# Three convolutions and an expert layer on one core: first image by ScalarE alone, group sums a pair later, scales ahead of the last low part, stores from ScalarE's queue

## The reference

```
x = x + conv3x3(gn(x), L0)         # 8 -> 8 channels, padding 1, bias
x = x + conv3x3(gn(x), L1)
x = x + experts(gn(x))             # axes (2, 8, 256, 256): 8 experts, 256 -> 1024 -> gelu -> 256
x = x + conv3x3(gn(x), L3)
```

## Time and profile before

| | us |
|---|---|
| median of 3 runs | 607.93 |
| profiled execution | 608.81 |
| its span in the profile | 607.0 |
| busy: TensorE / VectorE / ScalarE / GpSimd | 532.9 / 382.4 / 266.7 / 159.5 |

### The profile page before, as it was taken

One profiled execution on the slowest core, in us unless ns is written; L12 is line 12 of the kernel. 1 busy time (PEld: TensorE's weight loads), 2 busy tenths in 40 slices (PEclk: granted clock), 3 DMA queues, 4 the chain that ended last, 5 costly groups with the idle time before them and its releaser, 6 DMA issues.

```text
span 607.0 us, 9074 instructions
## 1 busy us (share of the span) xinstructions
PE 532.9 (88%) x3312; PEld 252.0 (42%) x3312; DVE 382.4 (63%) x658; ACT 266.7 (44%) x311; POOL 159.5 (26%) x168
## 2 busy tenths in 40 slices
PE   1565697999888999999999999999999997878984
PEld 0321242445454544444444444444444454544431
DVE  4996485999987549339158085193491638788533
ACT  0366348772353545336145163352461543665510
POOL 3744366997436000000000000000000000566520
PEclk9997797999979999999999999999999998979998
DMA  8724035554231022110120111011100000034678
GB/s 338 284 75 102 26 88 137 127 141 107 75 129 70 1 70 70 70 30 39 69 69 9 60 69 69 0 69 69 65 4 1 0 1 1 23 82 104 209 246 305
DMA packets 12293, 53.18 MB, mean 88 GB/s; under 512 B 2908, under 2 KB 3036, under 8 KB 9308
## 3 DMA queue, kind: packets, MB, share of 16 engines
q1 hardware_dynamic: 11976, 52.22, 26.7%
q10 hardware_dynamic: 288, 0.57, 0.3%
HBM read 25.83 MB, written 8.39 MB: 56 GB/s over the span
## 4 chain that ended last, share of the span: by engine, by line
PE 63%; DVE 21%; POOL 6%; SPq 3%; issue 2%; DMA 2%; ACT 1%; POOLq 0%; ACTq 0%; DVEq 0%
PE PS L952 27%; PE PS L931 25%; DVE ST L586 9%; PE PS L833 4%; POOL XN L365 4%; DVE X L624 4%; PE PS L840 3%; SPq L256 3%; DVE X L640 2%; DVE XT L633 2%; DVE PRE L651 1%; PE PS L908 1%; DMA X<-x 1%; PE PS L892 1%; DVE HID L724 1%
## 5 line engine op out<-in xcount | busy, mean ns | idle before, releaser
L931 PE MATMUL PS<-XT,W1S 128*128 (+1 forms) x768 | 171.8, 382 | 3.9 <-DVE W1S L647 3.7
L952 PE MATMUL PS<-HID,W2S 128*128 128x512 f16 x768 | 171.0, 380 | 1.6 <-DVE W2S L647 1.6
L486 ACT ACTIVATE SCR<-PS,CONST 128x512 f32<-128x512 f32 x128 | 87.3, 688 | 73.2 <-PE PS L931 37.1
L931 PEld LDWEIGHTS PS<-XT,W1S 128*128 128x128 f16 x768 | 75.5, 99 | 93.1 <-issue 7.0
L952 PEld LDWEIGHTS PS<-HID,W2S 128*128 128x128 f16 x768 | 75.4, 99 | 88.5 <-issue 2.4
L724 DVE SCALAR_TENSOR_TENSOR HID<-SCR,HID 128x512 f16<-128x512 f32 x128 | 88.5, 691 | 14.1 <-ACT HID L507 10.0
L365 POOL TENSOR_TENSOR XN<-SCR,XN 128x1024 f16<-128x1024 f32 x44 | 90.4, 2070 | 18.9 <-ACT SCR L454 18.6
L586 DVE BATCH_NORM_STATS2 ST<-X 128x6 f32<-128x512 f32 x128 | 86.3, 690 | 10.7 <-DMA X<-x 7.3
L647 DVE SCALAR_TENSOR_TENSOR W2S<-W2F,W2S 128x2048 f16<-128x2048 f32 x8 | 18.3, 2292 | 118.6 <-ACT W2S L482 118.6
L448 ACT ACTIVATE XN<-X,SC 128x1024 f16<-128x1024 f32 (+1 forms) x49 | 59.1, 1214 | 75.0 <-POOL SC L351 75.0
L624 DVE SCALAR_TENSOR_TENSOR X<-PS,X 128x512 f32<-128x512 f32 x96 | 64.9, 679 | 42.1 <-PE PS L854 41.7
(11 more groups left out here) (43 smaller groups left out, 401.5 us busy)
## 6 DMA issues: line engine op xcount, KB each, us to landing
W1F<-w SPq DMA_DIRECT2D x8, 1024.0 KB, 4.8
W2F<-w SPq DMA_DIRECT2D x8, 1024.0 KB, 4.8
HALO<-XN SPq DMA_DIRECT2D x48, 129.9 KB
out<-X SPq DMA_DIRECT2D x3, 2048.0 KB, 7.0
HALO<-XN SPq DMA_DIRECT2D x48, 121.8 KB
X<-x SPq DMA_DIRECT2D x2, 2048.0 KB, 18.9
HALO<-XN SPq DMA_DIRECT2D x48, 64.9 KB
HALO<-XN SPq DMA_DIRECT2D x48, 60.9 KB
```

The source lines that it names most:

```text
L486: act.activation(SCR[:, ft % 2, 0:CH], bank(ft % G_RING), ACT.Gelu, bias=BT[:, ds(e * FT + ft, 1)], scale=1.0 / (XS * WS)).then_inc(gelu_o ...
L931: mm = pe.matmul(bank(ft % G_RING), W1S[:, w, h * NF + ft * P:h * NF + (ft + 1) * P], rhs, start=(n == 0), stop=(n == 3 * DH - 1))
L952: mm = pe.matmul(bank(G2_BANK + h), W2S[:, w, ft * NW + h * P:ft * NW + (h + 1) * P], HID[p][:, part, ft], start=(ft == 0 and part == 0 an ...
```

## The change

It touches four places. (1) Image 0 is normalised like the others: ScalarE writes whole values to SCR too, `first_whole` goes, and the four loads of image 0 have 3, 2, 2 and 1 chunks. (2) In steps 2 to 7, `group_mean` stands behind pair 2 and not pair 1 on TensorE, `group_variance` behind pair 3 and not 2; VectorE's `deviation` and `variance` move from behind chunks 1 and 3 to behind 3 and 5. (3) GpSimd's list gets one rule for steps 0 to 7: all low parts of step g but the last, `scale_and_bias(g + 1)`, the last low part; the prepared chunks follow when all is done. (4) The stores of images 0 to 2 go, in halves of 1 MB, into ScalarE's list: image 0's halves behind its second and fourth piece of step 11, the other four behind those. SyncE keeps the eight stores of image 3.

```diff
+X0_CUTS = (0, 3, 5, 7, 8)
...
         for k in range(4):
-            load_image(0, k * NT // 4, (k + 1) * NT // 4, x0_in[k])
+            load_image(0, TC * X0_CUTS[k], TC * X0_CUTS[k + 1], x0_in[k])
...
             halos(g)
-            if g >= 9:
-                sp.wait_ge(x_new, X_NEW_AT["c", g - 1, NCH - 1])
-                store_image(g - 9, 0, NT)
         for i in range(NCH):
             sp.wait_ge(x_new, X_NEW_AT["c", 11, i])
-            store_image(NB - 1, TC * i, TC * (i + 1))
-        sp.wait_ge(out_done, 16 * (NB - 1 + NCH))
+            sp.dma_start(out[NB - 1][:, i * CH:(i + 1) * CH], x_chunk(NB - 1, i)
+                         ).then_inc(out_done, 16)
+        sp.wait_ge(out_done, 16 * (2 * (NB - 1) + NCH))
...
-        low_parts(0)
-        scale_and_bias(1)
-        low_parts(1, 0, 3)
-        scale_and_bias(2)
-        low_parts(1, 3)
...
-        pre_chunk(0)
-        pre_chunk(1)
-        low_parts(7, 3)
-        for j in range(2, NCH):
+        for g in range(8):
+            low_parts(g, 0, -1)
+            scale_and_bias(g + 1)
+            low_parts(g, -1)
+        for j in range(NCH):
             pre_chunk(j)
...
-            if g > 0:
-                if m >= FIRST_PIECE[1] + 2:
-                    act.wait_ge(lo_ok, m - 1)
-                act.activation(SCR[:, m % 2, 0:n * CH], src, ACT.Identity,
-                               bias=SC[:, k, 1:2], scale=SC[:, k, 0:1]).then_inc(xn_ok, 1)
+            if m >= 2:
+                act.wait_ge(lo_ok, m - 1)
+            act.activation(SCR[:, m % 2, 0:n * CH], src, ACT.Identity,
+                           bias=SC[:, k, 1:2], scale=SC[:, k, 0:1]).then_inc(xn_ok, 1)
...
-        for g in range(9, 12):
+
+        def store_half(b, i):
+            act.wait_ge(x_new, X_NEW_AT["c", 8 + b, i + NCH // 2 - 1])
+            act.dma_start(out[b][:, i * CH:(i + NCH // 2) * CH], x_chunk(b, i, NCH // 2)
+                          ).then_inc(out_done, 16)
+
+        for g in range(9, 11):
             normalise(g)
+        slot_free(11)
+        for k in range(NPR):
+            normalise_piece(FIRST_PIECE[11] + k)
+            if k % 2:
+                store_half(0, NPR * (k // 2))
+        for b in range(1, NB - 1):
+            for i in range(0, NCH, NCH // 2):
+                store_half(b, i)
...
-        dve.wait_ge(norm_ok, 1)
-        for i in range(NCH):
-            first_whole(i)
...
-                if i == 1 and g >= 2:
+                if i == 3 and g >= 2:
                     deviation(3 + g)
-                if i == 3 and g >= 2:
+                if i == 5 and g >= 2:
                     variance(3 + g)
...
-                if g >= 2 and k == 1:
+                if g >= 2 and k == 2:
                     group_mean(3 + g)
-                if g >= 2 and k == 2:
+                if g >= 2 and k == 3:
                     group_variance(3 + g)
```

37 lines of the change are left out of this document (5 added, 32 removed).

## The result

The changed kernel takes 615.38 us (median of 4 runs, 615.23 to 617.87), the kernel before 608.64 beside it (4 runs, 606.98 to 610.66): ratio 1.0119, 95% interval 1.0077 to 1.0161. It is slower, by about 7 us; the forecast was 605.0. The profiled execution took 615.27 us and is near its median, as is that of before.

What follows compares the result with a forecast made beforehand. It took TensorE and VectorE as about equally loaded in steps 2 to 7, losing time where both stand still, and the store drain as the end's bound. The front +0.4 and Part 5 -3.3 took 607.93 to 605.0 us; range 600.3 to 609.3.

Steps and rivals of the forecast that it cites:

- Part 1: First image normalised by ScalarE alone: first centre matmul waits for the row of ones anyway; 0 us (-0.3 to +0.5).
- Part 2: `scale_and_bias(1)` ahead of image 0's last low part: halos late for step 0's chunk 4; +1.3 us (0.7 to 2.5).
- Part 3: Step 3's low parts ahead of `scale_and_bias(4)`: TensorE's halo stall near 96 us goes; -6.9 us (at least 5.5, at most 7.2).
- Part 4: Later sums, prepared chunks behind the last low part: at step 6 only -0.6 of -5.6 us left; +1.0 more after.
- rival D: Step 3's stall stays because ScalarE's pieces are late; step 6 begins at 144.1 us, total 611.9 us; chance 0.05.
- (7,0): Transposes behind pair 0 of step 7, which wait for later prepared chunks; +1.0 us (0.4 to 2.5).
- The front: Convolution steps 0 to 7, before the expert stage, Part 1 to Part 4 together; +0.4 us (-2.4 to +2.5).
- Part 5: At the end, stores leave SyncE's queue, so step 11's halo copies start earlier and stores fill DMA gaps; -3.3 us.
- 597: Sign at the end: the prediction is wrong if the halos of step 11 land after 597 us.
- Rival C: At the end, all sixteen halo copies issue at 1.4 us, landing 3 us late; +4.1, total 612.4 us; chance 0.10.
- B: At the end, ScalarE's store backlog slows SyncE's issues to 1.38 us; tail -0.5, total 607.9 us; chance 0.17.
- my sum: Part 5's DMA drain: 23.3 us from 579.3, last byte at about 603.1, span 603.5 where it was 607.0.

Runs made afterwards that it cites:

- scale(1) behind: The changed kernel with `scale_and_bias(1)` behind image 0's last low part again, all else as changed; 610.76 us, ratio 1.0055 to the kernel before.

## Why the prediction was wrong

**Part 1 (0)** is right: -0.12% with an interval over zero; the first centre matmul is at 25.34.

**Part 2 (+1.3, up to 2.5): mis-sized; it measured 3.9.** Its steps came true: low part over at 37.55 (said 38.13), wait of 3.77 us for the copies (3), VectorE at 47.21 (46.5 at half clock). But I stopped at chunk 4. VectorE lost 0.67 us once more and its aggregate of image 3 came 2.8 us later (55.88 for 53.04). Step 2 began 5.7 us late. Taking part 2 back gave 3.9 us by the ratio and 3.55 at step 2 in the trace; the other 2.1 us stay in "scale(1) behind" and come, as far as one trace tells, with the held-up deviation of step 1, which is part 3's.

**Part 3 (-6.9) is right in its cause.** The stall is gone, and alone it is worth 0.90%, 5.5 us, the lower bound I gave. Of the 6.9, the 0.7 for shorter waits for a variance was wrong: those waits grew. And it has a price that I put at nothing. The low parts of step 3 that now go ahead of `scale_and_bias(4)` lie where VectorE forms the deviation in step 1: TensorE waited 3.73 us there instead of 2.60, and half clock followed where it hadn't before.

**Part 4 (leaves -0.6 of -5.6 at step 6) failed in its starting point.** From TensorE's end of step 5 to VectorE's step 6 it said 137.2 - 128.0 = 9.2 us, with 4.0 idle and half clock; measured 143.73 - 134.82 = 8.9, with 3.73 idle and half clock. But TensorE was done at 134.82, not 128.0: 4.35 of that is step 2's late start (5.65 in this trace for 1.3), and the rest the two waits, 1.41 and 1.29 us, where I took 0.74 away. The deviation falls where GpSimd runs a low part, and I priced an instruction of 0.22 us that took 2. The order of the low parts does that as well as the later sums: with the sums back, two deviations still take 1.47 and 1.59 us, though TensorE waits only 0.91 and 1.03 for them. The row was there: in the kernel before the same operation took 0.98 us at 84.02 and 0.87 at 114.78, against 0.22 in nine of its sixteen places. That step 6 began at 143.73, beside rival D's 144.1, is chance: D's cause, a stall left in step 3, wasn't there.

The Trainium skill (SBUF — State Buffer, "Who interferes with whom") bears on this term: a VectorE instruction with two SBUF inputs contends with a GpSimd instruction that reads SBUF, and one with at most one SBUF input, outside the two-port modes, does not. The trace agrees, with 1.99 us, until the low part's end, for the form with two tensor inputs and 0.27 for the other.

Judged alone, the sums cost 5.7 us. What I had as a hidden trade (their 2.85 us against slack that part 3 made) was a loss in full: with the sums in place part 3 keeps all its gain. At (7,0) I said +1.0; it is +0.5 (step 6 took 17.2 us for 16.7).

**The front (+0.4)** is +6.5 at the first expert matmul, +3.4 at step 8. The 3.1 between are clock and the chance place of one deviation, which another execution need not return.

**Part 5 (-3.3): the premise failed.** I said that the copies would go at 0.6 us each once no store stood ahead of them in their queue. They went at up to 1.85, beside 4 MB that ScalarE issued between 580.15 and 585.7, and landed at 599.44, past the 597 that I had named as a sign of being wrong. Rival C had the mechanism and nearly the size (last update 8 us later and +4.1 on the span; measured 7.3 and +3.1 beyond the front), but I gave it 0.10 and set it on the forecast's front. Rivals B and C priced the backlog at 1.38 us a copy, the row of a single 2 MB store. From the first issue to the landing the first eight copies took 17.0 us, where before they took 10.1: 3.0 of the 6.9 more are slower issues, and 3.8 are the last copy's landing (6.29 us for 2.46), for which B had 2.9 and no row. The other reading under B, that the copies keep half of the engines, isn't borne out either: between 588 and 596 us SyncE's queue had 24.9% of the engines' time and moved 0.51 of 2.77 MB, some 64 GB/s, where 154 went while the copies ran alone before. The rule of the Trainium skill that I set against the part (DMA: Bandwidth & Descriptors, "Issuing engines are not separate DMA queues": DMAs of several engines interleave, only issue time is saved) was nearer than my sum, though it would have given zero. The sum was also loose in itself: 579.3 + 23.3 is 602.6 and not 603.1, and 607.0 - 603.5 is 3.5 and not 3.3. What decided is how much is issued at once. Over all traces the end takes 58.6 to 59.4 us with ScalarE's backlog, 55.7 to 56.8 with SyncE's 2 MB stores as before, and 51.6 to 53.5 with ScalarE's stores spread out, so with the same queue the part is a gain (the changed kernel at 0.9968, for 1.0119 with the backlog and 1.0047 with the old stores).

The range failed with these. Part 2 and the front as a whole lay beyond the edges that I had given them (3.9 for at most 2.5, and 6.5 for at most 2.5). Part 5's +3.1 lay inside its widest edge, about +4, but that edge was rival C's and was left out of the range.
